# The last y of the previous image taken behind the first scan, a ring of ten slots, and a re-laid order of side steps

## The reference

```python
# --- layer 0: 3x3 convolution ---
x = x + _L0_conv_ref(_gn(x), ...)
# --- layer 1: 1x1 conv, state space model over 1024 tokens in four directions, 1x1 conv ---
def step(h, inp):                       # 16 states for each of 256 inner channels
    dt_t, B_t, C_t, u_t = inp
    dA = jnp.exp(dt_t[..., None] * A)
    h = dA * h + (dt_t * u_t)[..., None] * B_t[:, None, :]
    y = jnp.einsum('bdn,bn->bd', h, C_t)
    return (h, y)
y = ys.transpose(1, 0, 2) + uc * Dp
y = y * jax.nn.silu(z)
# --- layer 2: row and column means, two small state space models over 32 tokens, gates ---
# --- layer 3: 1x1 conv to 4 angles, a 4-qubit circuit, 1x1 conv back ---
```

## Time and profile before

| | us |
|---|---|
| three runs | 14577.62, 14580.07, 14580.96 |
| median | 14580.07 |
| profiled execution, its own time | 14580.03 |
| its span, first to last instruction | 14577.8 |
| POOL busy | 13621.9 (93%) |
| DVE busy | 13080.3 (90%) |
| PE busy | 12533.0 (86%) |
| ACT busy | 9797.4 (67%) |
| one image of the loop | 447.07 |

### The profile page before, as it was taken

How to read it: one execution, slowest core, us unless ns; L and a number is a source line. 1 busy time by engine, 2 the same in 40 slices (tenths; PEclk the granted TensorE clock), 3 DMA queues, 4 the chain that set the end, 5 groups by cost and what they waited for, 6 DMA issues and landing times.

```text
span 14577.8 us, 192392 instructions
## 1 busy us (share of the span) xinstructions
PE 12533.0 (86%) x60956; PEld 7802.1 (54%) x60956; DVE 13080.3 (90%) x8941; ACT 9797.4 (67%) x12092; POOL 13621.9 (93%) x4234
## 2 busy tenths in 40 slices
PE   6888888888888888888888888888888888888886
PEld 3555555555555555555555555555555555555554
DVE  6999999999999999999999999999999999999996
ACT  4666766667667677666676676766666666667664
POOL 6999999999999999999999999999999999999995
PEclk8999999999999999999999999999999999999997
DMA  4656556556556565565555665655655556655553
GB/s 169 232 219 225 223 221 228 222 222 225 219 225 228 219 225 223 220 232 221 222 226 218 228 226 218 227 219 222 232 218 228 219 222 228 225 220 224 221 221 123
DMA packets 582384, 3200.87 MB, mean 220 GB/s; under 512 B 65874, under 2 KB 65882, under 8 KB 319074
## 3 DMA queue, kind: packets, MB, share of 16 engines
q1 hardware_dynamic: 581346, 3187.71, 58.1%
HBM read 3107.75 MB, written 29.36 MB: 215 GB/s over the span
## 4 chain that ended last, share of the span: by engine, by line
POOL 35%; issue 22%; PE 21%; DVE 14%; ACT 4%; POOLq 0%; DVEq 0%; DMA 0%; ACTq 0%; SPq 0%
POOL ring L921 24%; PE work L1407 11%; POOL ring L904 10%; DVE ring L1395 8%; PE y_acc L1422 5%; DVE slot L1384 4%; PE y_acc L1407 3%; PE slot L1407 2%; ACT ring L1094 1%; ACT L937 1%; ACT u_conv L976 0%; DVE yz L1205 0%; ACT du L996 0%; DVE padded L1263 0%; POOL gn L865 0%
## 5 line engine op out<-in xcount | busy, mean ns | idle before, releaser
L921 POOL TENSOR_TENSOR ring<-ring,c_rows 128x2048 f32<-128x2048 f32 x2048 | 9290.3, 4542 | 654.2 <-DVE ring L1395 654.0
L1395 DVE TENSOR_TENSOR_SCAN ring<-ring,slot 128x1024 f32<-128x1024 f32 x2304 | 5265.6, 2285 | 242.9 <-ACT slot L1094 14.3
L1422 PE MATMUL y_acc<-wk,ring 128*128 128x128 f32 x32768 | 4511.4, 286 | 497.3 <-POOL ring L921 435.2
L1422 PEld LDWEIGHTS y_acc<-wk,ring 128*128 128x128 f32 x32768 | 3993.2, 149 | 1734.4 <-POOL ring L921 769.4
L904 POOL TENSOR_TENSOR ring<-du,b_rows 128x1024 f32<-128x1024 f32 x1792 | 4248.8, 2372 | 67.3 <-DVE du L1201 59.4
L1395 DVE TENSOR_TENSOR_SCAN ring<-slot,ring 128x1024 f32<-128x1024 f32 x1792 | 4074.8, 2274 | 167.3 <-POOL ring L904 148.9
L1094 ACT ACTIVATE slot<-dt,a_neg 128x1024 f32<-128x1024 f32 x1792 | 1995.6, 1114 | 1583.2 <-DVE ring L1395 1578.5
L1384 DVE TENSOR_TENSOR slot<-du,slot 128x1024 f32<-128x1024 f32 x2304 | 2789.6, 1211 | 104.5 <-PE slot L1407 100.4
L1094 ACT ACTIVATE ring<-dt,a_neg 128x1024 f32<-128x1024 f32 x2304 | 2591.6, 1138 | 155.0 <-issue 100.7
L1407 PE MATMUL slot<-stack,sel 96*128 96x512 bf16 x4608 | 1489.7, 407 | 854.5 <-DVE ring L1395 848.6
L1407 PE MATMUL work<-h_new,fused 128*128 128x512 f32 x4096 | 2093.6, 633 | 6.4 <-ACT u_conv L976 1.5
(11 more groups left out here) (173 smaller groups left out, 10117.0 us busy)
## 6 DMA issues: line engine op xcount, KB each, us to landing
c_rows<-cb_rows_scratch SPq DMA_DIRECT2D x2048, 1024.0 KB, 4.7
b_rows<-cb_rows_scratch SPq DMA_DIRECT2D x1792, 512.0 KB, 5.5
x_next<-in_x SPq DMA_DIRECT2D x32, 512.0 KB, 5.5
x_new<-x_next SPq DMA_DIRECT2D x32, 512.0 KB, 6.7
h_old<-h_new SPq DMA_DIRECT2D x32, 512.0 KB, 2.9
x_old<-x_new SPq DMA_DIRECT2D x32, 512.0 KB, 6.7
out<-x_old SPq DMA_DIRECT2D x32, 512.0 KB, 2.7
cb_rows_scratch<-stack SPq DMA_DIRECT2D x128, 96.0 KB
```

Source lines behind the costliest of these rows:

```text
L921: pool.tensor_tensor(pair, pair, c_rows[:, k % CB_BUFS, :, :], ALU.mult).then_inc(prod_ready, 1)
L1395: dve.tensor_tensor_scan(slot, a, b, 0.0, MUL, ADD).then_inc(scan_done, 1)
L1422: ins = pe.matmul(chunk(out_t, j), chunk(x, j), kc("ident"), is_transpose=True, start=start and j % (BANK // P) == 0, stop=stop, skip_grou ...
```

## The change

Four edits:
- `mix` : the step `("take", "before")` now comes after `("sum", -1)`, and `lay` starts with an end for that sum (the time at which PE is free at the plan's start). So the planner knows that the image in front is not summed up at once.
- `RING` goes from 8 to 10. As 128 units are no multiple of 10, the image's first units wait for the last unit of the image in front that had their slot (`slot_before`): units 0 to 7 still come eight units after it, units 8 and 9 ten after it, on a slot that was not used by the last eight.
- `x_new` is no tile of SBUF any more, but a tensor in device memory; that makes room for the two slots. The two copies of an image stay, one now writes to device memory and one reads from it.
- `PACE`, `WITHIN`, `SHIFTS` and four rows of `KINDS` are new. There are still 72 D and 56 P units.

```diff
-RING = 8
+RING = 10
-KINDS = ("DPDPDPDDDPDPDPDP", "DPDDDPDPDPDDDPDP", "DPDPDPDPDPDPDPDP", "DPDPDPDPDPDPDPDP",
-         "DPDPDPDDDPDPDPDP", "DPDPDPDPDPDPDPDP", "DPDPDDDPDDDPDPDP", "DPDPDDDPDDDPDPDP")
+KINDS = ("DPDPDPDDDPDPDPDP", "DPDPDDDPDDDPDPDP", "DPDPDPDPDPDPDPDP", "DPDPDPDPDPDPDPDP",
+         "DPDPDPDDDPDPDPDP", "DPDPDPDPDPDPDPDP", "DPDDDPDPDPDDDPDP", "DPDDDPDPDPDDDPDP")
...
-    steps = [step(("take", "before"), "D")] + turn_y("before", 1, 1)
+    steps = [step(("take", "before"), "D", None, [("sum", -1)])] + turn_y("before", 1, 1)
...
-PACE, WITHIN = 3.29, 0.22
+PACE, WITHIN = 3.02, 0.21
 SHIFTS = [
-    (50, -200, -237, -119, -232, -117, -214, -655, -609, -370, -396, -138, 15, -324, -226, -503, -430, -315, -279,
+    (13, 73, 142, 1, -290, -223, -495, -337, -66, -25, -372, -556, -595, -418, -265, -357, -331, -340, -403, -358,
...
+def slot_before(u):
+
+    return u - RING if u >= RING else max(v for v in range(UNITS) if v % RING == u) - UNITS
...
-    end, free, at = {}, dict(dict.fromkeys("PADG", 0.) if kind == "first" else LAG), dict.fromkeys("PADG", 0)
+    free, at = dict(dict.fromkeys("PADG", 0.) if kind == "first" else LAG), dict.fromkeys("PADG", 0)
+    end = {("sum", -1): free["P"]}
...
+        x_new = nc.dram_tensor("x_new_scratch", [P, TOK], F32).ap()
...
-        x_new = sb("x_new", [P, TOK])
...
-            sp.dma_start(x_new[:, :], x_next[:, :]).then_inc(x_moved, 16)
+            sp.dma_start(x_new, x_next[:, :]).then_inc(x_moved, 16)
...
-                        sp.dma_start(x_old[:, :], x_new[:, :]).then_inc(x_kept, 16)
+                        sp.dma_start(x_old[:, :], x_new).then_inc(x_kept, 16)
...
-                        pool.wait_ge(sum_done, s * UNITS + u - RING + 1)
+                        pool.wait_ge(sum_done, s * UNITS + slot_before(u) + 1)
...
-                            act.wait_ge(sum_done, s * UNITS + u - RING + 1)
+                            act.wait_ge(sum_done, s * UNITS + slot_before(u) + 1)
```

## The result

| | us |
|---|---|
| before, median of 4 runs | 14579.2 (14577.62 to 14580.96) |
| after, median of 4 runs | 14447.5 (14440.43 to 14454.21) |
| ratio | 0.991, 95% interval 0.9892 to 0.9927 |

The change saves 132 us, 0.9%. The forecast was 14314 us, 266 us less than before. So the sign is right, and half of the gain did not come: 133 us. The time still lies in the range of 14180 to 14480, at its upper end.

What follows compares the result with a forecast made beforehand. The prediction took POOL, waiting for DVE's scans, to bound the kernel. From 14580.0 us it took 234 for the image start and 32 for units 48 to 75, giving 14314 us; 8-in-10 range 14180 to 14480.

Steps and rivals of the forecast that it cites:

- ACT's gap of 4.5 us: After the jump back, ACT's first decay starts 4.61 us after its last work; forecast to stay, at about 4.6 us.
- ring and x_new: Ten slots instead of eight, and x_new in device memory: each forecast to be worth 0 by itself.
- So I lay the start of image 16 out anew, with the distances from the rows: scan 0 at 7272.1: Image start with the take behind scan 0: POOL's waits fall from 10.5 to 2.7 us, 7.8 per image, -234 us in all.
- DVE pays for its jump: Rival at the loop's jump back: DVE's jump delays scan 0 by 0.9 us, 26 us in 29 jumps, giving 14340; within the range.
- The term of -1.05 us per image: Units 48 to 75: DVE's 1.05 us wait for layer 2's first C row goes away, 30 by 1.05, -32 us.
- Nothing moves: Rival: DVE's saved time is lost at the next late thing within units 0 to 9; 14550 to 14580, chance 7%.
- more comes back: Rival: the waits of units 48 to 75 halve too; 14190, chance 9%.
- the wall: Rival, units 10 to 47: late PE work makes POOL wait 9.9 us per image, 297 us; 14611, slower, chance 7%.
- The new order gives part of it back: Rival: the new plan is wrong elsewhere, above all in units 48 to 75, 4 us per image; 14434, chance 17%.
- its two terms: The forecast's own range: start 5.8 to 9.4 us per image, units 48 to 75 from 4 less to 2 more.
- the rival that was taken into the range: The 14434 case, The new order gives part of it back; the range took in most of both neighbouring rivals.

Runs made afterwards that it cites:

- the second experiment: The kernel before with ten slots and x_new in device memory, its plan still made as if for eight slots: 14578.9 us, ratio 0.9999.
- The experiment with the tail put back: The changed kernel with the loop body's late dt_add put ahead of the next image's unit 0 spread, and its logarithm ahead of an ACT copy: 14377.2 us.
- The first experiment: The kernel before with only the take moved behind the scan of unit 0 in the loop body: 14478.7 us, ratio 0.9932.
- the hint: The changed kernel with an instruction atop each engine's loop body, meant to fetch the jump back's target code ahead: 14375.7 us, ratio 0.9861.
- the kernel with both edits: The changed kernel with dt_add and its logarithm moved earlier, and the loop's first instructions fetched ahead of the jump back: 14275.1 us, ratio 0.9792.
- the ninth experiment: The changed kernel with one more DVE reduction per image that nobody reads, ahead of outer_h in unit 69: 14490.2 us, ratio 0.9939.

## Why the prediction was right and wrong

**Right: what bounds, and what the take does.** POOL's wait for scans is what the change moves: 145 us less waiting, 132 us less time, POOL's own work as before. The take behind scan 0 waits no more, the four waits at the start became one large one, and the dt_u steps in front of units 9 and 16 wait for nothing. ACT's gap of 4.5 us stays. There is no wall in units 10 to 47 (0.00 us), and ring and x_new are worth 0 (the second experiment).

**Wrong: where scan 0 starts.** The failed step is "So I lay the start of image 16 out anew, with the distances from the rows: scan 0 at 7272.1". It has two pieces. From the end of the old image's last scan (7265.90, the dt_u at 7266.35 less its wait of 0.45) to the end of the last dt_u (7267.04) it took 1.14 us, as in the trace of before. In after the same piece is 7199.35 to 7204.09, 4.74 us: 3.60 more. From there to scan 0 it took 5.06 us, with ACT's gap and nothing for DVE's. In after it is 7204.09 to 7209.62, 5.53 us: 0.47 more. Image 16 is one of the better ones. Over images 2 to 30 the two pieces are 4.94 and 5.75 us in the mean, 3.80 and 0.69 more than I laid out. For the loop's 29 jumps back these are 110 and 20 us, 130 together. The entry into the loop is not among them: POOL's first wait is 1.0 us there.
- **The 110 us are the late dt.** I took the old image's tail from the trace of before, but the new plan had moved `dt_add` behind a spread and a sum. I had looked at which dt_u steps move, not at whether the last of them still gets its dt in time. The experiment with the tail put back takes the first piece from 4.94 to 2.40 us (1.14 were laid), while the second grows from 5.75 to 6.51, so scan 0 starts 1.8 us sooner, 52 us in 29 images; most of the rest of that run's gain lies in units 48 to 75. The first experiment has the new place of the take with the old tail: its last scan ends at 7217.58 and scan 0 starts at 7223.57, 5.99 us later, where I had laid 6.2; the mean over the images is 6.73. With the tail as it was the layout holds to half a microsecond.
- **PE's clock has a share in it that no run takes apart.** At the lower clock the spread and the sum ahead of `dt_add` take 1.3 us more than they took at the full one just before (2.95 for 1.64), which is an estimate of the share. In before PE was at the lower clock for a part of that stretch too (0.64 granted from 7257 to 7263).
- **The 20 us are DVE's jump,** which I had set at nothing in the sum with a bound of 26 us (the rival *DVE pays for its jump*). Its gap is 4.39 us in the mean, nearly ACT's 4.46, but the two jumps run side by side, so that only what DVE's exceeds ACT's path by is lost. The first experiment says about the same: 0.53 us above the layout, 15 us.

What the hint takes off, 72 us, is mostly no part of the miss, since the forecast kept ACT's gap and counted it. It is why the kernel with both edits, 14275 us, is 39 us under the forecast: scan 0 starts 3.7 us behind the last scan there. I had looked at that gap as a given.

By the Trainium skill (Runtime: NRT & Kernel Launch, Instruction fetch mechanics) a taken branch out of the window at hand stalls for its code; the trace agrees, with a mean of 4.4 us on DVE in after (127.4 by 29), 4.8 in the first experiment and none at the entry to image 31. The Trainium skill (Advanced Engine Details and Errata, Control Flow Timing) gives 108 ns for a compare-and-branch; with the hint 0.24 us of gap are left, which is nearer to it, and a jump without one is far from it.

**Wrong in size: units 48 to 75.** The term of -1.05 us per image was the wait of DVE for PE at the small model's C rows. That wait did go down: DVE's waits of this kind are 71.9 us in after, and they were 101.6 (1.0 us per image). But POOL's waits in that stretch rose by 1.56 us, and only the waits behind it, in units 76 to 127, fell, by 1.89. Over units 48 to 127 the gain is 0.33 us, not 1.05; 0.72 by 29 is 21 us. The largest rise is in POOL's wait at units 68 to 71, from 2.7 to 6.1 us. DVE's side steps between the scans of units 68 and 72 were 1.4 us per image in before and are 5.0 in after. That DVE's work at this place counts in full the ninth experiment shows. But it is not the whole cause. In before 4.2 us of side steps stood just ahead, in front of unit 67, so that units 67 to 72 hold 5.5 us of them in before and 6.2 in after. And the kernel with the tail put back has the same 6.2 us there, yet POOL's wait is 4.3 us, and its gain over units 48 to 127 is 1.64 us per image, more than the 1.05. So the loss goes with the late tail; by which way it reaches so far into the image stays open. (PE's granted clock over units 48 to 75 is 0.92 in after and 0.95 with the tail put back. The figures of this paragraph are sums of the timelines over images 2 to 30, divided by the images, as in the table.)

**The sum.** 130 for the start and 21 for the stretch are 151 us. In the profiled executions image 1's first product to image 31's first product took 13409.5 us in before and 13288.6 in after: 121 less, where 266 were forecast, so 145 are missing there. The images outside of the loop brought 5 us that I had not forecast, and the profiled execution of after is 7 us slower than its median; that leaves the 133. The 6 us between 151 and 145 are not explained. The forecast's own range has an error too: its two terms at their bounds give 14178 to 14466, not 14200 to 14450. And that the time lies within 14180 to 14480 is owed to the rival that was taken into the range, not to the layout.

**The rivals.** *Nothing moves*, *more comes back* and *the wall* fell. *The new order gives part of it back* (14434) has nearly the measured time, and for half of the reason it gave: a plan can be late at a new place. It looked for that place in units 48 to 75, and most of it was at the seam of two images.

## What to carry to other kernels

When a wait goes away, lay out what stood hidden under it before you price the gain: here a jump of over 4 us on DVE lay under a wait of 6.3 us, and moving one step made it visible. When a whole order is laid anew, follow the chain of the step that you expect to be next from its first link in the new order, not from the old trace. In a loop body a branch hint on each engine is cheap, and its worth is what no other wait covers: 33 us in one order of the same work and 72 in the other, or 110 where the take had been moved.

## What the runs showed of the hardware

- A jump back to the start of a long loop body (some 275 DVE and 380 ACT instructions per image) leaves a gap on DVE of 4.2 to 5.2 us (means of 29 jumps in six kernels) and on ACT of 4.1 to 5.0 us (means in eight kernels), in which the engine issues nothing. It starts when the engine reaches the jump, so it adds to a wait ahead of it (4.04 and 4.17 us in a row in after), and hides under one behind it (the take's waits in before are 207.4 us with the gap and 208.7 without). Going on past the loop without the jump leaves 0.04 us.
- An instruction at the top of the body that names the target takes DVE's gap to 0.24 us and ACT's to 0.13.
- PE stood still for 2.8 us, and its granted clock was 1.00 before, 0.51 in the 7 us that followed (the lower level, 1.2 GHz); eight matmuls of a sum took 1.92 us there and 1.04 at full clock.
- The same DVE reduction of 128x1024 numbers, 1.22 us long, cost 43 us in one place (1.4 us per image) and some 18 us (0.6) in a place where DVE is ahead.
